# Down projection in single-pass products with split inner values, and three first-half projections cut into parts

## The reference

```python
scores = jnp.einsum('bhqd,bhkd->bhqk', Q, K) / math.sqrt(D)      # D = 16
top_vals, _ = jax.lax.top_k(scores, U)                            # U = 31
scores = jnp.where(scores < top_vals[..., -1:], -jnp.inf, scores)
context = softmax(scores) @ V;   x = layernorm(x + context @ Wo.T + bo)
gate = jnp.einsum('bsd,hd->bsh', x, wg);  up = jnp.einsum('bsd,hd->bsh', x, wu)
x = layernorm(x + jnp.einsum('bsh,dh->bsd', silu(gate) * up, wd)) # 768 inner values
```

## Time and profile before

| what | value |
|---|---|
| median of three runs | 2994.08 us (2985.15 to 2994.3) |
| profiled execution: time, span | 3002.92 us, 3001.1 us |
| busy share PE, DVE, ACT, POOL | 90%, 83%, 83%, 79% |
| mean granted PE clock | 0.959 of full speed |

### The profile page before, as it was taken

How to read it: one execution, slowest core, us unless ns; L and a number is a source line. 1 busy time by engine, 2 the same in 40 slices (tenths; PEclk the granted TensorE clock), 3 DMA queues, 4 the chain that set the end, 5 groups by cost and what they waited for, 6 DMA issues and landing times.

```text
span 3001.1 us, 81706 instructions
## 1 busy us (share of the span) xinstructions
PE 2705.3 (90%) x21375; PEld 1449.9 (48%) x21375; DVE 2499.2 (83%) x12312; ACT 2478.7 (83%) x5890; POOL 2385.7 (79%) x1668
## 2 busy tenths in 40 slices
PE   5889999989998988899999999999988999899897
PEld 2444544545454444454545455454444545455455
DVE  5888888888889878888898988878888888888883
ACT  4888898888898877888888988878978888888883
POOL 1887888888798876787888888787877879778783
PEclk7899999999999989899999999999999999999998
DMA  3201111020111101111011110211101111110100
GB/s 88 48 21 42 25 41 38 24 49 26 37 30 36 42 21 37 29 29 45 23 42 25 41 39 24 47 27 37 30 25 45 26 40 27 32 42 23 37 2 22
DMA packets 91162, 102.67 MB, mean 34 GB/s; under 512 B 34529, under 2 KB 52962, under 8 KB 90594
## 3 DMA queue, kind: packets, MB, share of 16 engines
q1 hardware_dynamic: 89874, 96.35, 13.4%
q10 hardware_dynamic: 720, 0.14, 0.0%
HBM read 20.86 MB, written 8.39 MB: 10 GB/s over the span
## 4 chain that ended last, share of the span: by engine, by line
PE 36%; DVE 18%; SPq 15%; issue 13%; POOL 8%; ACT 6%; DMA 2%; DVEq 1%; ACTq 0%; POOLq 0%
SPq L386 8%; SPq L385 7%; DVE cand L941 7%; POOL mask L1219 6%; PE bench L740 5%; PE Y_ps L664 5%; PE ST_ps L684 4%; PE Y_ps L661 3%; PE ctxT_ps L698 3%; DVE S L934 3%; PE bench L734 3%; PE bench L605 3%; PE Y_ps L662 3%; PE ST_ps L681 3%; ACT junk L492 2%
## 5 line engine op out<-in xcount | busy, mean ns | idle before, releaser
L1219 POOL TENSOR_SCALAR mask<-S,thr,mb 128x512 bf16<-128x512 f32 x1015 | 2098.4, 2080 | 44.1 <-POOL mb L1213 33.5
L941 DVE MAX8 cand<-Y_ps 128x8 f32<-128x128 f32 x4096 | 1072.0, 282 | 7.4 <-issue 6.9
L492 ACT ACTIVATE junk<-S,at_zero,slope 128x512 bf16<-128x512 f32 x1024 | 824.7, 805 | 99.3 <-DVE S L934 99.2
L934 DVE TENSOR_SCALAR_CACHE_REDUCE S<-S_ps,na 128x512 f32<-128x512 f32 x1024 | 755.9, 738 | 170.7 <-PE S_ps L651 153.2
L502 ACT ACTIVATE above<-S,s,steep 128x512 bf16<-128x512 f32 x1024 | 824.6, 805 | 0.6
L510 ACT ACTIVATE PT<-ST_ps 128x512 f32<-128x512 f32 x1024 | 595.9, 582 | 193.0 <-PE ST_ps L684 187.4
L661 PE MATMUL Y_ps<-ones_b,nbig 128*128 128x512 bf16 x1024 | 403.0, 394 | 169.6 <-DVE cand L941 155.9
L651 PE MATMUL S_ps<-KS,QS 64*128 64x512 f32 x1024 | 523.0, 511 | 4.5 <-DVE S L934 2.3
L664 PE MATMUL Y_ps<-KS,QS 64*128 64x512 f32 x1024 | 523.0, 511 | 0.0
L684 PEld LDWEIGHTS ST_ps<-nbig,mask 128*128 128x128 bf16 x4096 | 235.8, 99 | 382.0 <-issue 382.0
L684 PE MATMUL ST_ps<-nbig,mask 128*128 128x128 bf16 x4096 | 414.8, 225 | 0.0
(11 more groups left out here) (187 smaller groups left out, 3684.6 us busy)
## 6 DMA issues: line engine op xcount, KB each, us to landing
QS<-Qhi SPq DMA_DIRECT2D x512, 32.0 KB, 2.0
KS<-Khi SPq DMA_DIRECT2D x512, 32.0 KB, 2.0
KS<-Klo SPq DMA_DIRECT2D x512, 32.0 KB, 2.0
QS<-Qlo SPq DMA_DIRECT2D x512, 32.0 KB, 2.0
xTs<-in_xT SPq DMA_DIRECT2D x17, 512.0 KB, 3.7
xs<-in_x SPq DMA_DIRECT2D x16, 512.0 KB, 3.9
out<-xs SPq DMA_DIRECT2D x15, 512.0 KB, 2.9
hT<-in_wgT SPq DMA_DIRECT2D x1, 768.0 KB
```

The costliest lines, as they stand in the source:

```text
L492: nc.scalar.activation(junk[:, :], S[:, score_place(j)[0], :], ACT.Tanh, bias=at_zero[:, :], scale=slope[:, hb, col:col + 1], accum_out=s0 ...
L934: nc.vector.tensor_scalar(S[:, at, :], S_ps[n % 2][:, :], na[:, hb, col:col + 1], None, ALU.add, op1=ALU.max, accum_out=rmax[:, n % RING:n ...
L941: mx = nc.vector.max(cand[:, j % CANDS, i, :], Y_ps[j % 2][:, i * BW:(i + 1) * BW])
L1219: nc.gpsimd.tensor_scalar(mask[:, h % MASKS, t, :], S[:, score_place(j)[0], :], thr[:, r:r + 1], mb[:, r:r + 1], ALU.is_lt, op1=ALU.add).t ...
```

## The change

1. The down projection. Inner values are no longer float32 in `hT`. POOL's product stays in `th`; ACT rounds it to the single-pass type `F32R` (`HIGH_SLOTS`), and DVE writes what the rounding left (`LOW_SLOTS`), also as `F32R`. Both parts live in `hS`, for the last two rounds in `x1T`. `wd` holds the integers themselves as `F32R`, and the factor 1/127 has moved to the copy of the up product. `narrow` runs twelve single-pass products for a tile of tokens instead of six float32 ones. The tail keeps float32 products. PE now waits for `h_split` ahead of slot 59; ACT's tanh waits for `h_split` where it waited for `h_done`.
2. `EARLIER`: the values product of slot 4 is made one tile of tokens at a time at slots 1, 2, 3 and 4, the query product half at slot 10 and half at 11, the key product half at 12 and half at 13. Each early part waits for the same `taken` count as the whole did.
3. To make room, some small tiles share the memory of `W`, and the integer weights are loaded through `mask` and `ups` at the start.

```diff
+EARLIER = {4: (1, 2, 3), 11: (2,), 13: (2,)}
+HIGH_SLOTS = {45: 0, 47: 1, 49: 2, 52: 3, 55: 4, 56: 5}
+LOW_SLOTS = {46: 0, 48: 1, 51: 2, 53: 3, 56: 4, 57: 5}
...
-        wd = sb("wd", [P, NF, DM])
+        wd = sb("wd", [P, NF, DM], F32R)
...
+        def h_part(i, f):
+            return hS[:, i, f, :] if f < NF - 2 else x1T[f - (NF - 2)][:, i, :]
...
                             if part > 1:
-                                act.wait_ge(h_done, (b - 1) * NF + part - 1)
+                                act.wait_ge(h_split, (b - 1) * NF + part - 1)
...
+                    if not first and not rest and n in HIGH_SLOTS:
+                        f = HIGH_SLOTS[n]
+                        act.wait_ge(h_done, (b - 1) * NF + f + 1)
+                        nc.scalar.activation(h_part(0, f), th[:, f % 2, :], ACT.Copy).then_inc(h_rounded, 1)
...
             def narrow(t):
                 for f in range(NF):
-                    mm = nc.tensor.matmul(bench[:, 0:DM], hT[:, f, t * P:(t + 1) * P], wd[:, f, :],
-                                          start=(f == 0), stop=(f == NF - 1))
+                    for i in range(2):
+                        mm = nc.tensor.matmul(bench[:, 0:DM], h_part(i, f)[:, t * P:(t + 1) * P], wd[:, f, :],
+                                              start=(f + i == 0), stop=(f + i == NF))
                 return mm
+            def ahead(b, n, first, rest):
+                for later, ends in EARLIER.items():
+                    i = n - later + len(ends)
+                    if not rest and 0 <= i < len(ends):
+                        t0, t1 = ends[i - 1] if i else 0, ends[i]
+                        what = HALF_USES[later]
+                        pe.wait_ge(taken, place(b, later, what, 0, first, rest))
+                        if what == "v":
+                            project_values(VALUES_AT.index(later), range(t0, t1))
+                        else:
+                            project("qk".index(what), 1, bench, slice(t0 * P, t1 * P))
...
                     if what == "down":
-                        pe.wait_ge(h_done, b * NF)
+                        pe.wait_ge(h_split, b * NF)
...
+                    if not first and not rest and n in LOW_SLOTS:
+                        f = LOW_SLOTS[n]
+                        dve.wait_ge(h_rounded, (b - 1) * NF + f + 1)
+                        nc.vector.tensor_tensor(h_part(1, f), th[:, f % 2, :], h_part(0, f).bitcast(F32),
+                                                ALU.subtract).then_inc(h_split, 1)
...
-                            nc.gpsimd.tensor_tensor(hT[:, part, :], th[:, part % 2, :], ups[:, :], ALU.mult).then_inc(h_done, 1)
+                            nc.gpsimd.tensor_tensor(th[:, part % 2, :], th[:, part % 2, :], ups[:, :], ALU.mult).then_inc(h_done, 1)
```

More of the change, by code:

```diff
@@ L177, in build @@
         ranks = sb("ranks", [P, RANKS])
-        ones = sb("ones", [1, P])
+        ones = sb("ones", [1, 1])
         ones_3 = sb("ones_3", [3, P], BF16)
@@ L256, in build @@
         W = sb("W", [P, L])
+        other, picked = (W[:, i * P:(i + 1) * P].rearrange("p (t r) -> p t r", t=PAIR) for i in range(2))
+        left = W[:, 2 * P:2 * P + 2 * BLOCKS * 8].rearrange("p (a e) -> p a e", a=2)
+        msq, rsd = (W[:, 320 + i * NT * HALF:320 + (i + 1) * NT * HALF] for i in range(2))
+        least, hidden = (W[:, 384 + i * PAIR:384 + (i + 1) * PAIR] for i in range(2))
         gtop = sb("gtop", [P, 4, 8])
         mask = sb("mask", [P, MASKS, NT, L], BF16)
+        ints = mask[:, :, :, :].rearrange("p m t l -> p (m t l)").bitcast(I32)
+        FAN = C * HID
         PT = sb("PT", [P, 4, L])
@@ L313, in build @@
         h_done = sem("h_done")
+        h_rounded = sem("h_rounded")
+        h_split = sem("h_split")
         out_done = sem("out_done")
@@ L373, in load_network @@
                 for i, src in ((0, wgT), (1, wuT)):
[L374 to L377, removed]
+                    sp.dma_start(ints[:, i * FAN:(i + 1) * FAN].rearrange("p (c n) -> p c n", c=C),
+                                 src.rearrange("(c p) n -> p c n", p=P)).then_inc(ffn_loaded, 16)
+                rows = wdT.rearrange("(c p) n -> p c n", p=P)
+                sp.dma_start(ints[:, 2 * FAN:2 * FAN + 4 * DM].rearrange("p (c n) -> p c n", c=4),
+                             rows[:, 0:4, :]).then_inc(ffn_loaded, 16)
+                sp.dma_start(ups[:, :].bitcast(I32).rearrange("p (c n) -> p c n", c=2),
+                             rows[:, 4:6, :]).then_inc(ffn_loaded, 16)
             def stack(h):
@@ L546, in slots @@
                                 act.wait_ge(h_done, (b - 1) * NF + part)
-                            nc.scalar.activation(ups[:, :], bench[:, :], ACT.Copy, scale=0.5 * DEQ * DEQ).then_inc(taken, 1)
+                            nc.scalar.activation(ups[:, :], bench[:, :], ACT.Copy, scale=0.5 * DEQ * DEQ * DEQ).then_inc(taken, 1)
                         if what in ("ctx_t", "x1_t"):
@@ L597, in _ @@
                     act.wait_ge(h_done, (B - 1) * NF + f)
-                nc.scalar.activation(ups[:, :], up[:, :], ACT.Copy, scale=0.5 * DEQ * DEQ).then_inc(last_ups, 1)
+                nc.scalar.activation(ups[:, :], up[:, :], ACT.Copy, scale=0.5 * DEQ * DEQ * DEQ).then_inc(last_ups, 1)
             normalised(B, 1, (0, 1), out_done)
@@ L602, in _, with project @@
         def _(pe):
-            def project(what, hb, to):
+            def project(what, hb, to, cols=slice(0, L)):
                 for c in range(C):
-                    mm = nc.tensor.matmul(to[:, :], wqk[what][:, c, hb * P:(hb + 1) * P], xTs[:, c, :],
+                    mm = nc.tensor.matmul(to[:, cols], wqk[what][:, c, hb * P:(hb + 1) * P], xTs[:, c, cols],
                                           start=(c == 0), stop=(c == C - 1))
@@ L629, in row_sums, with project_values @@
                 return mm
-            def project_values(g2):
+            def project_values(g2, tiles=range(NT)):
                 w = 2 * HG * D
-                for t in range(NT):
+                for t in tiles:
                     o = bench[:, t * w:(t + 1) * w]
@@ L739, in narrow @@
                 for f in range(NF):
-                    mm = nc.tensor.matmul(bench[:, 0:DM], hT[:, f, t * P:(t + 1) * P], wd[:, f, :],
-                                          start=(f == 0), stop=(f == NF - 1))
-                return mm
+                    for i in range(2):
+                        mm = nc.tensor.matmul(bench[:, 0:DM], h_part(i, f)[:, t * P:(t + 1) * P], wd[:, f, :],
+                                              start=(f + i == 0), stop=(f + i == NF))
+                return mm
+            def ahead(b, n, first, rest):
[9 more added lines that the diff above has]
+                            project("qk".index(what), 1, bench, slice(t0 * P, t1 * P))
             def on_bench(b, n, first, rest):
+                ahead(b, n, first, rest)
                 for what, part in uses_of(n, first, rest):
@@ L752, in on_bench @@
                     if what == "v":
-                        mm = project_values(VALUES_AT.index(n))
+                        mm = project_values(VALUES_AT.index(n), range(EARLIER[n][-1] if n in EARLIER else 0, NT))
                     if what in ("q", "k"):
@@ L756, in on_bench @@
                             pe.wait_ge(xT_loaded, (b + 2) * 16)
-                        mm = project("qk".index(what), 1 if n < VALUES_AT[1] else 0, bench)
+                        mm = project("qk".index(what), 1 if n < VALUES_AT[1] else 0, bench,
+                                     slice(EARLIER[n][-1] * P if n in EARLIER else 0, L))
                     if what == "keys":
```

26 lines of the change are left out of this document (10 added, 16 removed).

## The result

| | before | after |
|---|---|---|
| median of the runs | 2994.08 us (5 runs, 2985.15 to 2998.82) | 2976.46 us (5 runs, 2974.87 to 2984.82) |
| profiled execution: time, span | 3002.92, 3001.1 us | 2976.45, 2974.7 us |
| mean granted PE clock | 0.959 | 0.957 |

The ratio is 0.9963, interval [0.9949, 0.9977]: 0.37%, or 11 us, faster. The forecast was 29 us. The medians of these five and five runs are 17.6 us apart, more than the interval allows; where the text speaks of a gain it goes by the ratio. In a later session the same kernel had 0.9987 [0.9975, 0.9999]. So the direction was right, and most of the gain is missing. The two profiled executions are 26 us apart, but the one of before lies 9 us above its median, which leaves 17 or 18 to account for in these traces.

The account below looks back on a forecast made before the run. No engine alone sets the time; PE sets the pace in slots 59 to 62. -60 + 13 + 22 - 9 + 5 = -29 us, so 2974 in the profiled execution's terms, predicted median 2965; own range 2945 to 2988.

Parts of the forecast that it names:

- The down projection, -60: Slots 59 to 62: twelve single passes at 0.13 us each; DVE late next, so 4.0 us a sequence over 15.
- Rival (2): Down projection: a single pass costs 0.17 to 0.20 us, set by loading weights; 2995 to 3010 us, chance 0.15.
- rival (1): New ACT and DVE work is hidden behind other engines' lateness or in moving waits; 2942 us, chance 0.21.
- Two late subtractions, +22: DVE, slots 56 and 57: two of 0.6 us paid in full plus 0.3 waiting for POOL, 1.5 us a sequence.
- The sign that I had named: The prediction would be wrong if, among other signs, DVE's subtractions last over 1.3 us.
- rival (3): Slower: DVE subtractions wait for POOL's whole instructions, up to 4 us a sequence, 3.3 taken; 3015 us, chance 0.17.
- Paid in full: Slots 56 and 57: DVE runs without gaps there, so both subtractions of 0.6 us lengthen the sequence.
- Six roundings, +13: ACT, slots 45 to 56: 0.58 us a copy, mostly hidden, 0.9 us late a sequence; +9 to +24.
- The four covered subtractions, nothing: DVE, slots 46, 48, 51 and 53: they fall where DVE waits for PE or ACT, so cost nothing beyond ACT's 0.9.
- Early parts, -4: Values at slots 1 to 3, -9 us; queries' early half at slot 10, +5; keys 0.
- Values: Early value products in slots 1 to 3 end about 1.2 us earlier for at most 8 products: -9 us.
- The halves: Early query half in slot 10 waits for DVE to take the context, 0.35 us a sequence, +5; keys 0.

Follow-up runs that it names:

- the one column: Changed kernel with the subtractions of slots 56 and 57 made over 1 of 512 columns: 2955.32 us, 0.9875.
- the first pair: Changed kernel without any early parts, 2985.36 us, against changed kernel with only the values made early, 2978.95 us.
- the moved subtraction: Changed kernel with the subtractions of slots 56 and 57 moved from ahead of the statistics to behind the evacuation: 2951.52 us, 0.9862.

## Why the prediction was right or wrong

**The down projection, -60.** The passes came out as forecast: 0.13 us each, DVE next in line, 4.0 us a sequence (17.7 to 13.65) wherever the clock holds. Rival (2), passes of 0.17 to 0.20, is out. So is rival (1), that the new work is hidden, for the places it had: slots 42 to 58 grew by 2.4 us.

**The clock, not in the sum.** This is the step that failed most: "Four tiles would give 4.4 us a sequence, but what gets late next is DVE" took PE's full speed for granted because the earlier trace rows had 1.00 there. I had the wait of 1.40 us just ahead of these slots, and added DVE work to it. In 10 of 15 sequences PE ran at half its clock for 3.4 us there; 0.85 us in each of nine of them gave back 8 of the 60.

**Two late subtractions, +22.** 9.5 less 7.8 is 1.7 us a sequence, +26. That the total came near is partly luck, for one term was wrong: I took 0.3 us of waiting for POOL over the two, and slot 56 alone has 0.9. I had read off a mask, which has one SBUF input, that POOL holds DVE up only for its first 0.6 us, and carried that over to POOL's product of two. The sign that I had named, a subtraction of over 1.3 us, did show: 1.64 in the median of slot 56. The subtractions of after bear out the first half: those that start 0.05 to 0.61 us into a mask of 2.08 us begin their work when it is 0.63 to 0.65 old, and those that start later in it take 0.67 to 0.70. There are two exceptions: once the mask waited instead (2.59 us), and once POOL's product started 0.02 us behind the subtraction, which took 1.83. The product is different: one that starts 0.18 to 0.53 us into its 1.28 begins its work only 1.15 to 1.19 us into it, and so does the one column. The Trainium skill ("SBUF — State Buffer", section "SBUF: two separate sides") has it that whichever starts first holds the shared ports for its whole instruction. I had set this aside; the traces agree to 0.1 us for POOL's product and not for its masks. Whether it is the number of SBUF inputs that makes the difference isn't shown, since product and mask differ in operation and output type too. So rival (3) had the right mechanism at one place, with 0.9 us a sequence and not 3.3.

"Paid in full" was true of this place, not of the work: behind the evacuation the same two cost 0.2 to 0.3 us a sequence. I had named what was queued behind them on DVE, but not what PE had queued behind the statistics: a product that writes `bench`, with all scores after it.

**Six roundings, +13.** 0.6 to 0.8 us in slots 42 to 55, +10. **The four covered subtractions, nothing.** Right; moving the only one of them that is regularly disturbed gained nothing measurable.

**Early parts, -4.** Values: forecast -9, measured -6 (2985.36 to 2978.95 us) and -8 (2950.18 to 2942.55). The number is right, the way to it is not. I had at most 8 sequences gain 1.2 us each; slots 0 to 8 got shorter in all 16 sequences of the first pair and in 15 of the second, by 1.2 in the median, and slots 9 to 16 gave back 0.7 to 0.8 on average. The halves: forecast +5, measured +9 and +12, the second term that was sized wrong. Together the early parts cost some 3 us (2 alone, 5 on top of the down projection) where -4 was forecast. In after, PE waits for the context taken (L1070) ahead of a query product, which it did not have to with whole products (engine, line, waited for: us, times, longest):

```profile
PE bench L624 <- DVE ctxs L1070: 14.0, 13, 7.9
```

One of them, 7.9 us long, lies in slot 10 of the thirteenth sequence, where PE waited 7.6 us for DVE in before too. Of the other twelve nine last 0.3 to 0.5 us, where 0.35 was forecast, and three about 1.0 to 1.2. So the wait alone doesn't explain 9 to 12 us; what else the halves cost isn't shown.

**The sum.** -60 + 8 + 26 + 10 + 3 = -13 us. The ratio says -11, the medians of the runs say -17.6, and the two traces are 26 us apart, 9 of them in the seventh sequence alone (207.1 us in before, 197.8 in after). So the sum is closed to some 5 us and no better. The first sequence is longer by 4.5 us in after (179.8 for 175.3). It is 175.8 to 179.8 in the traces of all changed kernels, early or not. What sets it was not tried, nor why the changed kernel's ratio differed between two sessions (0.9963 and 0.9987); its clock fell in 13 sequences of the second trace.

**What was shown and what not.** That the place of two instructions costs about 1% is shown by runs. That of it 0.6 to 0.8 us a sequence is the collision is shown by the one column (8.4 less 7.8) and by moving slot 56's alone (9.5 less 8.7). That the longer wait of PE causes the fall of the clock is borne out by the order of these fourteen traces only, and within one trace the wait doesn't sort the sequences: I changed the wait through DVE's work each time, and never filled it with work for PE.

## What to carry to other kernels

When work is added to an engine that another waits for, look in that slot's program for the first instruction behind which the other engine's whole queue stands, and put the work past it, best into a hole that is called "issue". Shortening products may not pay in full if the same change lengthens the wait ahead of them: check the granted clock there as well as the busy time. An instruction that is undisturbed beside one instruction of another engine proves nothing about its contention with a different one: a mask and a product of POOL held DVE up by different spans.

## What the runs showed of the hardware

- POOL's product of two SBUF inputs (1.28 us) holds a DVE subtraction up for 0.9 us even where that has one column; a DVE instruction of one input and 32 columns ended with the second of two subtractions of POOL back to back, after 2.93 us instead of 0.17. A mask (2.08 us) holds a subtraction up only until it is 0.63 to 0.65 us old; one that was 0.59 us old cost it 0.05.
- PE's clock fell to half in slots 57 to 60, for 3.4 us, in some sequences 6.8, behind mean idle times of 1.70 us and more in 10 to 15 of 15 sequences, behind 1.37 and less in 0 to 2.
- POOL waits as well: the mask that starts right behind the product, with DVE's subtraction just begun, took 2.51 us in after, and 2.08 beside the moved subtraction.
